# Splitting the graph stage's 64 expert calls between its first and its last part

## The reference

```python
# x: 8192 tokens of 64 numbers, 262144 edges between tokens (plus one loop each)
h = (x @ W_gat).reshape(M, HEADS, NUM_EXPERTS)
a_src, a_dst = (h * att_src).sum(-1), (h * att_dst).sum(-1)
e = leaky_relu(a_src[src] + a_dst[dst], 0.2)
alpha = softmax of e over the edges that end in the same token
agg = segment_sum(h[src] * alpha, dst) + b_gat
scores = layernorm(agg).mean over heads        # one number for each expert
w = softmax of the two highest scores
for ei in range(NUM_EXPERTS):                  # 4 experts
    hh = gelu(x @ W1[ei] + b1[ei])             # 64 -> 128
    out += gate[ei] * (hh @ W2[ei] + b2[ei])   # 128 -> 64
```

## Time and profile before

| | |
|---|---|
| time, median of 3 runs | 10232.95 us (10220.48 to 10233.31) |
| the profiled execution's own time | 10221.47 us |
| its span, first to last instruction | 10219.7 us |
| mean granted TensorE clock | 0.909 of full speed |
| busy: PE, DVE, ACT, POOL | 79%, 75%, 50%, 67% of the span |
| graph stage | 7447 to 9349 us of the span |

### The profile page before, as it was taken

One profiled execution on the slowest core, in us unless ns is written; L12 is line 12 of the kernel. 1 busy time (PEld: TensorE's weight loads), 2 busy tenths in 40 slices (PEclk: granted clock), 3 DMA queues, 4 the chain that ended last, 5 costly groups with the idle time before them and its releaser, 6 DMA issues. The chain is left out here.

```text
span 10219.7 us, 112146 instructions
## 1 busy us (share of the span) xinstructions
PE 8073.3 (79%) x34375; PEld 3937.8 (39%) x34375; DVE 7633.6 (75%) x6810; ACT 5138.6 (50%) x6133; POOL 6829.2 (67%) x3866
## 2 busy tenths in 40 slices
PE   0158888888888888888888879799749999985769
PEld 0123333333333333333333333233237777753522
DVE  8769999999999999999999953477735655534144
ACT  0046666666666666666666623367615554421123
POOL 0059999999999999999999963300067777761047
PEclk9679999999999999999999988699969999965579
DMA  0057677677767766666676740000032222210022
GB/s 10 0 138 182 175 179 180 178 178 177 180 175 178 181 177 177 180 177 177 177 181 175 178 87 1 11 1 1 1 35 29 27 29 27 27 17 5 0 71 89
DMA packets 385896, 1064.96 MB, mean 104 GB/s; under 512 B 106434, under 2 KB 129602, under 8 KB 383378
## 3 DMA queue, kind: packets, MB, share of 16 engines
q1 hardware_dynamic: 338482, 1044.16, 39.8%
q0 software_dynamic: 47136, 17.04, 3.8%
HBM read 995.98 MB, written 63.50 MB: 104 GB/s over the span
## 5 line engine op out<-in xcount | busy, mean ns | idle before, releaser
L535 POOL TENSOR_TENSOR hC<-h,Cb 128x1024 f32<-128x1024 f32 x1536 | 3600.9, 2357 | 434.6 <-DVE h L630 413.7
L630 DVE TENSOR_TENSOR_SCAN h<-dA,B_ps 128x1024 f32<-128x1024 f32 x1344 | 3073.1, 2287 | 156.4
L308 PE MATMUL y_ps<-hC,con 128*128 128x512 f32 x6144 | 2969.9, 606 | 80.5 <-DVE gz L636 80.3
L455 ACT ACTIVATE dA<-delta,negA 128x1024 f32<-128x1024 f32 x1344 | 1535.3, 1145 | 1204.6 <-DVE h L630 1200.3
L616 DVE TENSOR_TENSOR B_ps<-dx,B_ps 128x1024 f32<-128x1024 f32 x1344 | 1623.9, 1208 | 166.3 <-PE B_ps L302 166.3
L308 PEld LDWEIGHTS y_ps<-hC,con 128*128 128x128 f32 x6144 | 1186.2, 194 | 1145.5 <-issue 943.2
L2626 POOL DMA_INDIRECT g_got<-scratch_node,g_idx x1152 | 1143.6, 993 | 359.8 <-issue 350.7
L302 PE MATMUL B_ps<-Bpart,sel 96*128 96x512 bf16 x2688 | 828.6, 390 | 648.0 <-DVE h L630 645.7
L2676 PE MATMUL g_pick<-g_third,g_hot 128*128 128x256 bf16 x10752 | 1260.9, 274 | 0.0
L2676 PEld LDWEIGHTS g_pick<-g_third,g_hot 128*128 128x128 bf16 x10752 | 1020.2, 98 | 203.8 <-issue 81.9
L2722 ACT ACTIVATE g_hot<-g_fill 128x512 bf16<-128x512 f32 x896 | 485.8, 594 | 653.2 <-PE g_fill L2659 651.5
(11 more groups left out here) (493 smaller groups left out, 11652.4 us busy)
## 6 DMA issues: line engine op xcount, KB each, us to landing
Cb<-scratch_c_rows SPq DMA_DIRECT2D x3072, 256.0 KB, 4.1
drive<-scratch_c_rows SPq DMA_DIRECT2D x384, 256.0 KB, 5.2
eb_share<-scratch_gate_rows SPq DMA_DIRECT2D x128, 256.0 KB, 3.5
scratch_c_rows<-BCrow SPq DMA_DIRECT2D x96, 256.0 KB, 4.0
scratch_edge<-g_out SPq DMA_DIRECT2D x64, 384.0 KB, 2.3
par<-in_ssm SPq DMA_DIRECT2D x48, 395.5 KB, 5.3
g_got<-scratch_node,g_idx POOLq DMA_INDIRECT x1152
scratch_place<-s_zero SPq DMA_DIRECT2D x4, 1024.0 KB, 11.1
```

The costliest lines, as they stand in the source:

```text
L308: last = nc.tensor.matmul(y_ps[:, hs], con[:, K_ID:K_ID + P], hC[k % DEEP][:, hs], start=(k == 0), stop=(k == STEPS - 1))
L455: A(dA[k % DEEP][:, :], delta[d][:, :], ACT.Exp, scale=negA[:, n:n + 1]).then_inc(decay_ready, 1)
L535: G.tensor_tensor(hC[k % DEEP][:, :], hst[k % DEEP][:, :], Cb[k % DEEP][:, :], ALU.mult).then_inc(prod_ready, 1)
L630: V.tensor_tensor_scan(hst[k % DEEP][:, ::step], decayed[:, ::step], driven[:, ::step], 0.0, ALU.mult, ALU.add).then_inc(scanned, 1)
```

## The change

22 of the 64 calls run in the first part of the graph stage, the other 42 in the last part. The code of a call is the same; it now stands in functions that take the range of calls. The counts of the five semaphores run on from the first part to the last one, so they belong to the whole stage. The weights are loaded in both parts. `rest` and `staged` move from tiles 0 to 7 of `y_all` to tiles 56 to 63, since the first 22 calls write tiles 0 to 23. `ad0` is cleared by VectorE instead of GpSimd. Apart from that, two semaphores of `EndSearch` become one (`made`), and one semaphore of the short block is merged into another.

```diff
+        w_loaded, h_ready, hid_ready, y_ready, y_kept = (
+            outer.enter_context(nc.semaphore("r_" + n)) for n in ("w_loaded", "h_ready", "hid_ready", "y_ready", "y_kept"))
+        CALLS, EARLY = GATES * (TILES // GROUP), 22
+
+        def load_experts(sp, tiles):
+            for dst, given in zip(tiles, experts):
+                sp.dma_start(whole(dst), given).then_inc(w_loaded, 16)
+
+        def call_experts(pe, tiles, calls):
+            win, wout, _, _, hid, ps_h, ps_y = tiles
+            def hidden(c):
+                if c >= 2:
+                    pe.wait_ge(hid_ready, c - 1)
+                nc.tensor.matmul(ps_h[c % 2][:, :], win[:, c % GATES, :], tnT_sb[:, c // GATES * HALF:(c // GATES + 1) * HALF],
+                                 start=True, stop=True).then_inc(h_ready, 1)
+            hidden(calls[0])
+            for c in calls:
+                if c + 1 in calls:
+                    hidden(c + 1)
+                pe.wait_ge(hid_ready, c + 1)
+                if c >= 2:
+                    pe.wait_ge(y_kept, c - 1)
+                for g in range(GROUP):
+                    last = nc.tensor.matmul(ps_y[c % 2][:, g * C:(g + 1) * C], hid[c % 2][:, g * P:(g + 1) * P],
+                                            wout[:, c % GATES, :], start=True, stop=True)
+                last.then_inc(y_ready, 1)
+
+        def gelu_experts(act, tiles, calls):
...
+        def keep_experts(dve, tiles, calls):
...
+            dve.wait_ge(y_kept, calls[-1] + 1)
@@ first part
+            tiles, early = expert_tiles(ctx, sb, "n"), range(EARLY)
-                NODE_ROWS = 6
+                NODE_ROWS = 7
                     sp.dma_start(t0[:, :], x["target0"]).then_inc(loaded, 16)
+                    load_experts(sp, tiles)
                     sp.wait_ge(link, NODE_ROWS)
...
-                    nc.gpsimd.memset(ad0[:, :], 0.0).then_inc(zeroed, 1)
-                    pool.wait_ge(zeroed, 1)
                     pool.wait_ge(loaded, 32)
                     pool.wait_ge(places_filled, 64)
-                    pool.wait_ge(link, 2)
+                    pool.wait_ge(link, 3)
...
+                @block.tensor
+                def _(pe):
+                    pe.wait_ge(w_loaded, 64)
+                    call_experts(pe, tiles, early)
+                @block.scalar
+                def _(act):
+                    act.wait_ge(w_loaded, 64)
+                    gelu_experts(act, tiles, early)
...
+                    link_(V.memset(ad0[:, :], 0.0))
                     dve.wait_ge(loaded, 32)
...
+                    dve.wait_ge(w_loaded, 64)
+                    keep_experts(dve, tiles, early)
@@ middle part
-            rest = y_all[:, 0:GATES, :]
+            rest = y_all[:, TILES - 2 * GATES:TILES - GATES, :]
-            staged = y_all[:, GATES:2 * GATES, :]
+            staged = y_all[:, TILES - GATES:TILES, :]
@@ last part
+            tiles, late = expert_tiles(ctx, sb, "j"), range(EARLY, CALLS)
...
-                    for c in range(CALLS):
...
+                    pe.wait_ge(w_loaded, 128)
+                    call_experts(pe, tiles, late)
...
+                    act.wait_ge(w_loaded, 128)
+                    gelu_experts(act, tiles, late)
...
+                    dve.wait_ge(w_loaded, 128)
+                    keep_experts(dve, tiles, late)
                     dve.wait_ge(taken, 16 * 2 * TILES)
```

More of the change, by code:

```diff
@@ L2313, in __init__ @@
         self.zero = sb("zero", [P, ECOLS])
-        self.marked, self.numbered, self.zeroed, self.idx_ready, self.shifted, self.link = (
-            sem(n) for n in ("marked", "numbered", "zeroed", "idx_ready", "shifted", "link"))
+        self.marked, self.made, self.idx_ready, self.shifted, self.link = (
+            sem(n) for n in ("marked", "made", "idx_ready", "shifted", "link"))
         self.branches, self.leaves = sem("branches"), sem("leaves")
@@ L2327, in number @@
     def number(self, pool):
-        self.nc.gpsimd.iota(self.node[:, :], pattern=[[P, TILES]], base=0, channel_multiplier=1).then_inc(self.numbered, 1)
-        self.nc.gpsimd.memset(self.zero[:, :], 0.0).then_inc(self.zeroed, 1)
+        self.nc.gpsimd.iota(self.node[:, :], pattern=[[P, TILES]], base=0, channel_multiplier=1).then_inc(self.made, 1)
+        self.nc.gpsimd.memset(self.zero[:, :], 0.0).then_inc(self.made, 1)
     def gather(self, pool, table, level, here):
@@ L2370, in first_level @@
         dve.wait_ge(self.marked, 16)
-        dve.wait_ge(self.numbered, 1)
+        dve.wait_ge(self.made, 1)
         self._count(dve, self.marks[:, :].unsqueeze(1).broadcast_to([P, TILES, FAN]))
@@ L2449, in graph_stage, with expert_tiles @@
         ad0 = keep_sb("ad0", [P, HEADS_G])
+        w_loaded, h_ready, hid_ready, y_ready, y_kept = (
+            outer.enter_context(nc.semaphore("r_" + n)) for n in ("w_loaded", "h_ready", "hid_ready", "y_ready", "y_kept"))
+        CALLS, EARLY = GATES * (TILES // GROUP), 22
+        def expert_tiles(ctx, sb, tag):
+            tiles = [sb("win", [C, GATES, P]), sb("wout", [P, GATES, C]), sb("b1", [P, GATES]), sb("b2", [P, GATES, C]),
+                     [sb(f"hid{k}", [P, HALF]) for k in range(2)]]
+            for n in ("ps_h", "ps_y"):
+                tiles.append([ctx.enter_context(nc.psum_tensor(f"{tag}_{n}{k}", [P, HALF], fp32)) for k in range(2)])
+            return tiles
@@ new lines, in gelu_experts @@
+        def gelu_experts(act, tiles, calls):
+            _, _, b1, _, hid, ps_h, _ = tiles
+            for c in calls:
+                act.wait_ge(h_ready, c + 1)
+                if c >= 2:
+                    act.wait_ge(y_ready, c - 1)
+                nc.scalar.activation(hid[c % 2][:, :], ps_h[c % 2][:, :], ACT.Gelu, bias=b1[:, c % GATES:c % GATES + 1]
+                                     ).then_inc(hid_ready, 1)
+        def keep_experts(dve, tiles, calls):
+            _, _, _, b2, _, _, ps_y = tiles
+            for c in calls:
+                turn, ex = c // GATES, c % GATES
+                dve.wait_ge(y_ready, c + 1)
+                nc.vector.tensor_tensor(y_all[:, turn * GROUP:(turn + 1) * GROUP, ex * C:(ex + 1) * C],
+                                        ps_y[c % 2][:, 0:GROUP * C].rearrange("p (g c) -> p g c", g=GROUP),
+                                        b2[:, ex, :].unsqueeze(1).broadcast_to([P, GROUP, C]), ALU.add).then_inc(y_kept, 1)
+            dve.wait_ge(y_kept, calls[-1] + 1)
@@ L2461, in graph_stage @@
             t0 = sb("t0", [P, 1], i32)
-            loaded, zeroed, link, rows_out, spread = (
-                sem(n) for n in ("loaded", "zeroed", "link", "rows_out", "spread"))
+            tiles, early = expert_tiles(ctx, sb, "n"), range(EARLY)
+            loaded, link, rows_out, spread = (sem(n) for n in ("loaded", "link", "rows_out", "spread"))
             with nc.Block() as block:
-                NODE_ROWS = 6
+                NODE_ROWS = 7
                 @block.sync
@@ L2907, in graph_stage @@
             ps2 = ctx.enter_context(nc.psum_tensor("k_ps2", [P, HALF], fp32))
-            loaded, link, pe_done, exp_done, out_done = sem("loaded"), sem("link"), sem("pe"), sem("exp"), sem("out")
+            loaded, link, pe_done, exp_done = sem("loaded"), sem("link"), sem("pe"), sem("exp")
             with nc.Block() as block:
@@ L2917, in _ @@
                     sp.wait_ge(link, LAST)
-                    sp.dma_start(carry_tbl, back[:, :]).then_inc(out_done, 16)
-                    sp.wait_ge(out_done, 16)
+                    sp.dma_start(carry_tbl, back[:, :]).then_inc(loaded, 16)
+                    sp.wait_ge(loaded, 48)
                 @block.tensor
@@ L3021, in _ @@
                 def _(sp):
-                    for dst, given in zip((win, wout, b1, b2), experts):
-                        sp.dma_start(whole(dst), given).then_inc(w_loaded, 16)
+                    load_experts(sp, tiles)
                 @block.tensor
                 def _(pe):
[L3027 to L3034, removed]
-                    for c in range(CALLS):
[L3036 to L3044, removed]
+                    pe.wait_ge(w_loaded, 128)
+                    call_experts(pe, tiles, late)
                 @block.gpsimd
```

14 lines of the change are left out of this document (3 added, 11 removed).

## The result

The changed kernel takes 10153.76 us (median; 10145.73 to 10160.15), the kernel before 10232.19 us in the same comparison. The profiled execution took 10145.73 us, its span 10143.9; against the profiled execution before that is 75.7 us less.

The account below looks back on a forecast made before the run. TensorE's calls were taken to bound the last part's first stretch, GpSimd's scatters and drain the first part. Subtracting 78.5 us gave 10143.0 from the profiled execution, 10154.5 from the median; the middle, 10149 us, was forecast, range 10137 to 10170.

Parts of the forecast that it names:

- The forecast (A): Whole kernel: the calls' move gains 78.5 us, other terms cost 0, giving 10149 us; chance 0.75.
- Calls taken out of the end: Last part: 22 calls fewer free 85.8 us, but the gathers then end last, so the gain is 78.5 us.
- Calls put into the first part: First part: 22 calls take 86.3 us and end 5 us before GpSimd's drain is over, so cost 0.
- Queues: First part: weight loads ahead of the table stores, keeps and the moved memset make nobody wait; cost 0.
- The table load: Middle part: ScalarE's first Exp needs a 1.28 us table load, covered for VectorE; cost 0, at most 1.3 us.
- Rival B: First part: each of 22 keeps stretches a scatter by 0.25 us, 5.5 us in all, about 10155; chance 0.07.
- Rival C: First part: TensorE's code or a weight load is delayed by the table stores, +4.3 to +13.6 us; chance 0.09.
- Rival D: Middle part: gather contention changes; small, 5 us either way, chance 0.06; large, at 0.1 us per gather 10264, chance 0.01.
- Rival E: First part: calls would not overlap with the scatters, so the 78.5 us come back, 10227; chance 0.02.
- The level: Whole kernel: starting times of 10221 and 10233 give 10143.0 and 10154.5; the middle, 10149 us, was taken.

Follow-up runs that it names:

- experiment 4: Changed kernel plus an unread VectorE instruction behind each of 22 early keeps: first part 97.8 us (short product), 98.3 (long product), 98.4 (copy), against 96.5.
- experiment 5: Changed kernel with softmax chain, top-2 gates and gated sum in two halves, the first between late calls' keeps: 10116.01 us, ratio 0.9881 to the kernel before.

## Why the prediction was right

**The forecast (A)** held: 10149 us was said and 10153.8 measured, and the gain of 78.5 us, worked out against the own time of the execution, is 78.8 in the part where it was placed and 78.4 in the medians. That the medians come so near is partly luck: the two profiled executions differ by 75.7 us, 2.8 less than forecast, mostly because the middle part took 3.6 us longer.

- *Calls taken out of the end.* Right, and by its own step: the gain is not 22 x 3.90 = 85.8 us, since the gathers end 7 us behind the calls. The idle time of 7.05 us ahead of L3147 is that difference, and the runs with 16 and 28 early calls show both sides of it. The prediction had 7.3.
- *Calls put into the first part.* Right to a tenth: 86.3 us from TensorE's first product to the last keep, in both. TensorE started 4.5 us after the part's start (7445.67 to 7450.21), where 4.7 was said. The slack against the drain was 5 us, and six more calls used it up and cost 18.3 us.
- *Queues.* No wait appeared: the node table's store was issued 8.6 us after the first small load, against 8.5 before.
- *The table load.* It stands where it was put, and is covered:

```profile
7605.56 1.28 ACT L2809 ACT_TABLE_LOAD   x1
...
7609.22 1.22 DVE L2899 TENSOR_TENSOR g_X<-g_got,g_X 128x512 f32<-128x512 f32 x1
```

The load is over at 7606.84, and the result is used first at 7609.22 with no idle time before it. The figure of 1283 ns from the Trainium skill (ScalarE: Activation LUTs, What ACT_TABLE_LOAD costs) agrees with this row. The drain that its page adds is not seen here: the Exp starts at 7606.85, 0.01 us after the load.

- *Rival B* did not happen for the keeps. All but the first two scatters take 0.97 to 0.98 us, though the keeps come 0.06 us later against the scatters with each call and so, over 22 calls, meet a scatter at every point of its run. The price of 0.25 us each, taken from the first two scatters, is not a fixed price even where two SBUF inputs contend: it is what was left of the VectorE instruction that the scatter met. The products of experiment 4 cost 0.25 us once, and 0.06 for each later one because the scatters fell into step.
- *Rival C* did not happen: TensorE is idle for 4.5 us until the weights are there and for 6.1 us behind its last product; in the 85.9 us between it is busy for 85.5. The calls kept their 3.90 us through the stretch in which the table stores land.
- *Rival D*, small, is within its bounds: +3.6 us in one pair of profiles, 2.7 of them seen with nothing changed. A large one did not come.
- *Rival E* did not happen.

**The level.** The prediction set its number between two levels of the time before, 10221 and 10233. The further runs fill the space between and around them: the later executions of the kernel before lie between 10231.4 and 10250.0 us, and the eight of the changed kernel at 10136.5, 10144.4, 10145.7, 10152.4, 10155.1, 10155.2, 10158.5 and 10160.2. It is a spread, not two levels, and much of it arises ahead of the graph stage, which began between 7440 and 7461 us. The middle of the two was a choice, not a derivation. 10149 lies 4.8 us below the first median of the changed kernel and 0.8 us below the second, 10149.8.

## What to carry to other kernels

Work moved out of a stage is worth at most the distance to the next thing that ends there, not its own length, and it is free where it lands only up to what ends last there: read both from one profile before choosing how much to move (here 21 to 23 calls of 64 by the rows, of which 22 was run, with 16 and 28 on either side). Count a queue's drain at the end of a block as part of the cover, here 5.4 us. When a stage is left waiting for indirect DMAs, fill the wait with halves of the work that follows, in short VectorE instructions, since a gather that meets one may wait for its end. And when a stall costs the same small amount in every round of a loop, compare the periods of the two engines before calling it a price: here 0.06 us was the difference between a call and three scatters.

## What the runs showed of the hardware

- An indirect DMA on GpSimd that starts inside a VectorE instruction with two SBUF inputs waits for its end. Each scatter that a product of experiment 4 made longer, of 0.68 or of 1.22 us, ended 0.84 to 0.86 us after that product, and the gather of 1.98 us in experiment 5 ended 0.87 us after one. Twenty-two such products added only 1.2 and 1.8 us over 64 scatters, because the scatters fell into step with the calls. An indirect DMA that had started 0.25 us before the product kept its 0.98 us.
- A one-input copy of 128x1024 held up scatters as well, 22 of them by 1.8 us over 64, and a scatter that had started 0.5 us before a copy took 1.30 us. Twenty-two keeps with one PSUM input cost nothing.
- GpSimd's drain at the end of the first part, where the engine has waited for its last indirect DMA to land, took 5355 ns in all ten profiles, whatever the others did. In the middle and the last part of the kernel before the drain was issued while gathers still ran, and took 21.7 and 14.3 us.
- The middle part with its 1152 gathers differs in length between executions of the same code: 1508.9 and 1511.6 us.
